# Cross-attention and gated-attention block on one core: a new instruction order on all five engines, with the column-strip products of two groups side by side

## What is computed

```python
def _L0_xattn_ref(x_q, x_kv, indices, W_q, W_kv_down, W_kv_up, W_out):
    q = (x_q @ W_q.T).reshape(b, nq, H, HD)          # 16 heads of 16
    c_kv = x_kv @ W_kv_down.T
    c_sel = c_kv[jnp.arange(b)[:, None, None], indices]   # 64 picks of 154 keys a row
    kv = (c_sel @ W_kv_up.T).reshape(b, nq, K, 2, H, HD)
    scores = jnp.einsum('bqhd,bqkhd->bqkh', q, kv[:, :, :, 0]) * SCALE
    attn = jax.nn.softmax(scores, axis=2)
    return jnp.einsum('bqkh,bqkhd->bqhd', attn, kv[:, :, :, 1]).reshape(b, nq, d) @ W_out.T
...
    # second layer: q1, k1, v, q2, k2 (softmax), gates gk1, gk2 (log-sigmoid / 16), router e
    o = o_dense + o_sparse      # chunked gated linear attention, dense and by expert (4, top 1)
    g = (x @ Wga @ Wgb).reshape(B, L, H, DV)
    o = o * lax.rsqrt(jnp.mean(o * o, axis=-1, keepdims=True) + EPS) * norm_w
    return (o * (g * jax.nn.sigmoid(g))).reshape(B, L, H * DV) @ Wo
x = x + _L0_xattn_ref(_layernorm(x, axis=-1), ctx_1024, itok_BxSx64_0_2047, ...)
x = x + _L0_ffn_ref(_layernorm(x, axis=-1), ...)
```

## Time and profile before

| | |
|---|---|
| median of 3 runs | 1111.31 us (1107.6 to 1114.18) |
| the profiled execution, its own time | 1110.09 us |
| its span, first to last instruction | 1108.8 us |
| mean granted TensorE clock | 0.982 |
| TensorE busy | 1052.0 us, 95% |
| VectorE busy | 956.1 us, 86% |
| ScalarE busy | 898.9 us, 81% |
| GpSimd busy | 698.4 us, 63% |

### The profile page before, as it was taken

The page is one execution under the profiler, slowest core; times in us unless marked ns, Lnnn a source line. Parts: engine busy times, 40 slices in busy tenths (PEclk is TensorE's granted clock), DMA queues, the critical chain, the costliest instruction groups (busy, mean ns, idle before and its releaser), DMA issues.

```text
span 1108.8 us, 36916 instructions
## 1 busy us (share of the span) xinstructions
PE 1052.0 (95%) x14912; PEld 871.9 (79%) x14912; DVE 956.1 (86%) x2793; ACT 898.9 (81%) x2259; POOL 698.4 (63%) x707
## 2 busy tenths in 40 slices
PE   4779999999999999999999999999999999999986
PEld 2557888888888888888888888888888888888764
DVE  5679999998999898999989989998999999998652
ACT  3478888888888888888888888888888888888762
POOL 5356666677765666776666667666667766665554
PEclk8689999999999999999999999999999999999999
DMA  6342322232222222223212222222222222121111
GB/s 199 104 127 59 75 55 63 54 87 63 66 69 52 58 67 67 64 67 89 57 47 62 64 63 73 75 61 67 61 57 68 59 70 59 49 60 50 32 32 25
DMA packets 86880, 74.21 MB, mean 67 GB/s; under 512 B 34553, under 2 KB 71743, under 8 KB 86710
## 3 DMA queue, kind: packets, MB, share of 16 engines
q1 hardware_dynamic: 86134, 70.85, 24.2%
q10 hardware_dynamic: 576, 1.02, 0.3%
HBM read 37.43 MB, written 13.94 MB: 46 GB/s over the span
## 4 chain that ended last, share of the span: by engine, by line
PE 73%; DVE 8%; DMA 5%; ACT 4%; POOL 4%; SPq 3%; issue 2%
PE F L410 9%; PE F L873 5%; PE TM L734 5%; PE F L818 5%; PE F L404 5%; PE F L884 4%; PE F L846 4%; PE F L786 4%; PE F L801 3%; PE F L878 3%; PE TM L743 3%; PE F L759 3%; PE F L829 2%; PE F L865 2%; PE SA L722 2%; PE TM L753 2%
## 5 line engine op out<-in xcount | busy, mean ns | idle before, releaser
L729 DVE CUSTOM_DVE_ANT_0 SA<-SA,LNC 128x154 f32<-128x154 f32 x512 | 146.4, 348 | 12.1 <-PE SA L722 12.1
L2128 POOL TENSOR_TENSOR LS<-LS,ZABS 128x512 f32<-128x512 f32 x27 | 47.4, 1755 | 152.0 <-ACT ZABS L1823 152.0
L734 PE MATMUL TM<-CONST,EXPS 128*128 128x128 f32 x512 | 90.0, 299 | 3.8 <-ACT OT L1735 2.3
L715 DVE TENSOR_REDUCE PACKED<-HOT 128x20 int32<-128x1280 bf16 (+1 forms) x64 | 91.7, 1433 | 0.0
L734 PEld LDWEIGHTS TM<-CONST,EXPS 128*128 128x128 f32 x512 | 72.0, 208 | 17.0 <-issue 12.8
L2118 POOL TENSOR_TENSOR LS<-LS,ZABS 128x1024 f32<-128x1024 f32 x27 | 63.9, 2365 | 33.0 <-ACT ZABS L1889 33.0
L729 DVE DVE_READ_ACCUMULATOR2_ANT MAXS<- 128x1 f32 x512 | 72.2, 141 | 0.0
L2143 POOL TENSOR_TENSOR QM<-QD,ISEXPT 128x1024 f32<-128x1024 f32 x27 | 64.1, 2373 | 5.9 <-DMA QD<-QG 5.9
L722 PE MATMUL SA<-KNOW,QS 128*128 128x154 bf16 x512 | 56.5, 233 | 11.0 <-DMA QS<-q_dram 5.9
L2145 POOL TENSOR_TENSOR AT<-AT 128x1024 f32<-128x1024 f32 x27 | 64.4, 2384 | 3.8 <-DVE AT L1460 3.8
L873 PE MATMUL F<-QM,STATE 128*32 128x128 f32 x2048 | 64.0, 278 | 2.5 <-POOL QM L2183 1.9
(11 more groups left out here) (536 smaller groups left out, 3796.8 us busy)
## 6 DMA issues: line engine op xcount, KB each, us to landing
QD<-QG SPq DMA_DIRECT2D x128, 128.0 KB, 2.3
QS<-q_dram SPq DMA_DIRECT2D x64, 192.0 KB, 3.0
q_dram<-QPARTS SPq DMA_DIRECT2D x32, 192.0 KB, 2.5
XA<-x_dram SPq DMA_DIRECT2D x32, 128.0 KB, 2.1
QS<-q_dram SPq DMA_DIRECT2D x32, 128.0 KB, 3.0
XB<-x_dram SPq DMA_DIRECT2D x32, 128.0 KB, 3.4
out_dram<-OUT SPq DMA_DIRECT2D x32, 128.0 KB, 1.7
EG<-EGP SPq DMA_DIRECT2D x128, 4.0 KB, 1.8
```

The costliest lines, as they stand in the source:

```text
L715: return dve.tensor_reduce(PACKED[:, r], HOT[:, r, :], AX.X, ALU.add)
L729: last = dve.tensor_tensor_reduce(s, s, LNC[t % 2][:, :], -1.0, LARGE, ALU.add, ALU.min, out[:, h:h + 1])
L734: pe.transpose(TA[:, cols(hh)], exps[:, 0:P, hh], ident)
```

## The change

No operation is added, removed or altered. The queues of all five engines are written in a new order, in the first, the middle and the last turns, and the semaphores and waits are drawn anew for it. The diff is 1,444 lines; this is its core, for the middle turns. On TensorE, lines that only rename a semaphore left out:

```diff
         def pe_tiles(l, a, b, c, d, e):
+            pe.wait_ge(s_d_q1, d + 1)
+            gate_products(LS3[d % 2], CUME[d % 2]).then_inc(s_d_g2_ps, 1)
             pe.wait_ge(s_c_xm, c + 1)
-            pe.wait_ge(s_a_xt, c + 3)
             transposes(C0, XM[:, :], KD).then_inc(s_c_xmt_ps, 1)
-            gate_products(LS3[d % 2], CUME[d % 2]).then_inc(s_d_g2_ps, 1)
+            pe.wait_ge(s_b_exps, 4 * b + 1)
+            exp_transposes(EXPS[:, 0]).then_inc(s_b_exps_ps, 1)
             scores(b, 1).then_inc(s_b_b, 1)
...
             hidden(XMT[c % 2]).then_inc(s_c_hidden_ps, 1)
-            exp_transposes(EXPS[:, 0]).then_inc(s_b_exps_ps, 1)
             pe.wait_ge(s_d_q2, d + 1)
             inner(KG1T, Q1).then_inc(s_d_a1_ps, 1)
...
+            pe.wait_ge(s_b_probs, 2 * b + 1)
+            exp_transposes(EXPS[:, 1]).then_inc(s_b_exps_ps, 1)
             pe.wait_ge(s_d_kg2_at1, 2 * d + 1)
-            exp_transposes(EXPS[:, 1]).then_inc(s_b_exps_ps, 1)
+            pe.wait_ge(s_b_exps_2, b + 1)
+            scores(b, 3).then_inc(s_b_b_3, 1)
             pe.wait_ge(s_d_kg2_at1, 2 * d + 2)
...
-            pe.wait_ge(s_b_exps_4, b + 1)
-            scores(b, 3).then_inc(s_b_b_3, 1)
...
             values_pair(b, 2).then_inc(s_b_values, 1)
-            pe.wait_ge(s_c_rt, c + 1)
-            pe.wait_ge(s_c_zmin, 2 * c + 2)
+            pe.wait_ge(s_d_0, d + 1)
+            dense_kv_products(V[d % 2]).then_inc(s_d_kvd_ps, 1)
+            pe.wait_ge(s_c_router_y, 2 * c + 2)
+            pe.wait_ge(s_c_zmin, c + 1)
             router_rows().then_inc(s_c_rows_ps, 1)
+            pe.wait_ge(s_d_sq, d + 1)
+            pe.matmul(D2, const("pairs"), RMS[:, :], start=True, stop=True).then_inc(s_d_ms_ps, 1)
+            pe.wait_ge(s_b_ot, 2 * b + 2)
+            transposes(TA, flat(OT[:, :, :]), GROUPS).then_inc(s_b_ot_ps, 1)
...
+            half_pairs_rows(MIDS, KIDS, WG, HID2, HIDG, WKB, HID1, HIDK).then_inc(s_c_k2_ps, 1)
...
             scores(a, 0).then_inc(s_b_scores, 1)
...
-            dense_kv_products(V[d % 2]).then_inc(s_d_ms_ps_kvd_ps, 1)
...
-            half_pairs_rows(MIDS, KIDS, WG, HID2, HIDG, WKB, HID1, HIDK).then_inc(s_c_k2_ps, 1)
```

On VectorE the K2 product goes ahead of QG2 and the weighting of HOT behind both; of the state halves, half 0 (bank D1) is added first, and LABB comes behind both:

```diff
+            dve.wait_ge(s_c_soft, 6 * d + 5)
+            dve.tensor_tensor(K2[d % 2][:, :, :], K2[d % 2][:, :, :], KS[:, 3, :].unsqueeze(2).to_broadcast([P, H, DK]), ALU.mult).then_inc(s_c_soft, 1)
             dve.wait_ge(s_d_q2_ps, d + 1)
             dve.scalar_tensor_tensor(two_halves(flat(QG2[:, :, :])), MIDD, DK ** -0.5, two_halves(EP[:, :]), ALU.mult, ALU.mult).then_inc(s_d_q2, 1)
...
             dve.wait_ge(s_d_o_ps, d + 1)
+            dve.tensor_tensor(state_half(0), state_half(0), F[:, 2, :], ALU.add).then_inc(s_d_0, 1)
+            dve.tensor_tensor(state_half(1), state_half(1), F[:, 3, :], ALU.add).then_inc(s_d_states, 1)
+            dve.tensor_copy(LABB[:, :], RT[:, 4:5]).then_inc(s_c_router_y, 1)
```

On ScalarE the copy of VM (0, 0) goes to the turn's start, and the fourth EXPS of the second group stands between HID1 and ZPARTS. On GpSimd, of the lane to `state_outputs`:

```diff
+            pool.wait_ge(s_d_egd, 64 * d + 64)
+            decays(d).then_inc(s_d_dec, 1)
             pool.wait_ge(s_c_zparts, 2 * c + 1)
             pool.tensor_tensor(ZREST[:, :], HID2[:, :], ZPARTS[:, 0, :], ALU.subtract).then_inc(s_c_zrest, 1)
```

and X1B is copied before SG, not behind it. On SP:

```diff
             z_slabs(0).then_inc(s_c_zslabs, 16)
+            sp.wait_ge(s_a_qrest, 2 * a + 2)
+            sp.dma_start(q_dram.rearrange("(n p) w -> p n w", n=PARTS), QPARTS[:, :, :, :].rearrange("p n k t -> p n (k t)")).then_inc(s_a_qstore, 16)
             z_slabs(1).then_inc(s_c_zslabs, 16)
             z_slabs(2).then_inc(s_c_zslabs, 16)
```

More of the change, by code:

```diff
@@ L1083, in pe_tiles @@
             values_pair(b, 2).then_inc(s_b_values, 1)
-            pe.wait_ge(s_c_rt, c + 1)
-            pe.wait_ge(s_c_zmin, 2 * c + 2)
+            pe.wait_ge(s_d_0, d + 1)
+            dense_kv_products(V[d % 2]).then_inc(s_d_kvd_ps, 1)
+            pe.wait_ge(s_c_router_y, 2 * c + 2)
+            pe.wait_ge(s_c_zmin, c + 1)
             router_rows().then_inc(s_c_rows_ps, 1)
+            pe.wait_ge(s_d_sq, d + 1)
+            pe.matmul(D2, const("pairs"), RMS[:, :], start=True, stop=True).then_inc(s_d_ms_ps, 1)
+            pe.wait_ge(s_b_ot, 2 * b + 2)
+            transposes(TA, flat(OT[:, :, :]), GROUPS).then_inc(s_b_ot_ps, 1)
+            pe.wait_ge(s_c_hidk, 16 * c + 16)
+            pe.wait_ge(s_c_hidg, 16 * c + 16)
+            pe.wait_ge(s_c_by_label, c + 1)
+            half_pairs_rows(MIDS, KIDS, WG, HID2, HIDG, WKB, HID1, HIDK).then_inc(s_c_k2_ps, 1)
             if a % TPB == 0:
@@ L1090, in pe_tiles @@
             scores(a, 0).then_inc(s_b_scores, 1)
-            pe.wait_ge(s_d_sq_norm, 2 * d + 1)
-            pe.wait_ge(s_d_states_0, 2 * d + 1)
-            pe.matmul(D2, const("pairs"), RMS[:, :], start=True, stop=True).then_inc(s_d_ms_ps_kvd_ps, 1)
-            pe.wait_ge(s_b_ot, 2 * b + 2)
-            transposes(TA, flat(OT[:, :, :]), GROUPS).then_inc(s_b_ot_ps, 1)
-            pe.wait_ge(s_d_states_0, 2 * d + 2)
-            dense_kv_products(V[d % 2]).then_inc(s_d_ms_ps_kvd_ps, 1)
-            pe.wait_ge(s_c_hidk, 16 * c + 16)
-            pe.wait_ge(s_c_hidg, 16 * c + 16)
-            pe.wait_ge(s_c_by_label_scan0, 2 * c + 1)
-            half_pairs_rows(MIDS, KIDS, WG, HID2, HIDG, WKB, HID1, HIDK).then_inc(s_c_k2_ps, 1)
             pe.wait_ge(s_b_out, 2 * b + 2)
@@ L1128, in pe_last_tiles @@
                 hidden(XMT[c % 2]).then_inc(s_c_hidden_ps, 1)
+            if b < TILES:
+                exp_transposes(EXPS[:, 0]).then_inc(s_b_exps_ps, 1)
             if d < TILES:
@@ new lines, in sp_first_tiles @@
+            sp.dma_start(XA[:, :], x[rows(l), :]).then_inc(s_l_load_xa, 16)
+            if l >= 1:
+                sp.wait_ge(s_a_index, l)
+            sp.dma_start(IDX[:, :], idx[rows(l), :]).then_inc(s_l_load_idx, 16)
+            if d >= 0:
+                sp.wait_ge(s_d_exp2, 2 * d + 1)
+                eg_move(d, 0, 1).then_inc(s_d_egd, 16)
+            if b == 0:
+                sp_weights2()
+            if d >= 0:
+                eg_move(d, 0, 0).then_inc(s_d_egd, 16)
+            if a == 0:
+                sp_after_first()
@@ L2225, in sp_first_tiles @@
             if c >= 0:
-                sp.dma_start(HIDK[0:DK, :], HID1[DK:P, :]).then_inc(s_c_hidk, 16)
+                sp.wait_ge(s_c_zstore, 32 * c + 32)
+                z_slabs(2).then_inc(s_c_zslabs, 16)
+            if a == 0:
+                sp_k_store_first()
+            if d >= 0:
+                sp.dma_start(QD[DK * 1:DK * 1 + DK, 0, :, :], QG2[DK * 0:DK * 0 + DK, :, :]).then_inc(s_d_qd, 16)
+            if c >= 0:
+                z_slabs(0).then_inc(s_c_zslabs, 16)
+                z_slabs(1).then_inc(s_c_zslabs, 16)
             if a >= 0:
@@ L2316, in sp_last_tiles @@
+                sp.dma_start(HIDK[0:DK, :], HID1[DK:P, :]).then_inc(s_c_hidk, 16)
                 sp.wait_ge(s_c_zrest, 2 * c + 2)
```

1420 lines of the change are left out of this document (694 added, 726 removed).

## The result

The changed kernel takes 1112.61 us (median of 20 runs, 1110.6 to 1120.39) against 1110.19 for the kernel before in the same comparison (1106.71 to 1114.18): ratio 1.0025, interval 1.0014 to 1.0036. It is slower by 2.4 us. That is less than the 0.5% (5.5 us) which the prediction took for the least that can be told from no change, but with 20 runs of each kernel the interval lies above 1: a small loss. The profiled execution has a span of 1111.9 us (1113.25 in all); its mean granted clock is 0.986, before 0.982, so the loss is not one of the clock.

The account below looks back on a forecast made before the run. TensorE, busy 95% of the span, was taken as the bound. 27 turns at −0.02 to +0.07 us give 0 ± 2; less 1 for the head, 1110.09 becomes 1109, rounded to 1110 us, range 1099 to 1127.

Parts of the forecast that it names:

- The seam: TensorE's cost of entering or leaving 32-column strip products; moving dense kv makes three into two, saving 0.13 us a turn.
- ffn_out to the turn's first group: TensorE segment closing the turn: gates ahead of XM's transposes hide the 0.26 us XM wait, 6.71 to 6.45 us.
- Start to the first inner product: TensorE segment opening the turn: EXPS transposes and gates earlier, new 0.12 us wait for QG, 5.02 to 4.79 us.
- First inner to state_outputs: TensorE segment: same groups reordered, some 0.2 us wait for GpSimd's second QM, 12.58 to 12.8 us.
- the slower rival: GpSimd's lane before state_outputs has no slack, so lateness is paid in full: 0.6 us a turn, 1126 us, chance 0.36.
- State outputs' end to ffn_out: TensorE segment: dense waits for D1, router for LABB, so the mean square starts later; 4.89 to 5.23 us.
- Sum of an undisturbed turn: Five TensorE segments of one steady main-loop turn added: 32.18 us against 32.11 before, +0.07.
- Irregular turns: Turns carrying extra waits: late QS loads gain 1.9 us of room, ZS waits count none; 0 to 0.1 us better.
- QS: Two late loads, 0.35 us each, before TensorE's scores; moving scores (a, 0) two groups later gives them 1.9 us more.
- Head: First turns: q loads no longer stand behind SP's W store; 1 us gained, bounds 0 and 5.
- Tail: Last five turns: counted at nothing, bounded by 1 us to either side.
- Signs: What the new profile would show if right: period 32.1 to 32.3 us, no XM wait, waits on LABB and OG.

Follow-up runs that it names:

- b_dense: Kernel before with only dense_kv_products moved directly behind values_pair(b, 2) and VectorE adding state half 0 first: 1120.46 us, ratio 1.0099.
- experiment 4: Changed kernel with DEC behind ZREST on GpSimd: 1112.82 us; the same with SyncE's middle turns in the old order: 1105.15 us.
- a_sp: Changed kernel with only SyncE's middle turns put back into their order of before: 1105.29 us, ratio 0.9955.
- a_qidx: Changed kernel with q_store behind the third ZS load and the IDX load ahead of the EG moves: 1107.76 us, ratio 0.9987.

## Why the prediction came out as it did, step by step

- **The seam**: 0.13 us a turn forecast; b_dense shows 0.13. Right, and its fate as well ("this is where the saved seam goes"). The estimate of 0.22 us a seam that the prediction drew from the Trainium skill, TensorE: Matmul & The Clock Gate, section Single matmul latency, was too high here. The prediction also feared, by the Trainium skill, TensorEngine Tiling (Array Packing), section PSUM Bottleneck, that emptying PSUM would hold the moved group back. No trace here shows that: dense starts 0.90 us (b_dense) and 0.89 us (changed kernel) after the state outputs' end, right behind the values groups, and the 0.1 us of wait for D1 that the prediction gave it is not there. What b_dense lost came behind dense, from the later mean square.
- **ffn_out to the turn's first group**: 6.45 forecast, 571.77 − 565.29 = 6.48. Right; no wait for XM is left.
- **Start to the first inner product**: 4.79 forecast, 4.99 measured. The wait for QG, put at 0.12, is 0.3 (543.39 to 544.70 less the 1.00 of hidden; TensorE's weights wait for QG 6.1 us in 18 turns). The term was mis-sized by 0.2. The four maxima were put at 0.48 us behind the start of scores (541.45); they start 0.85 behind it, because VectorE is still at the step before:

```profile
541.74 0.65 DVE L1429 TENSOR_SCALAR KS<-KS,RT 128x8 f32<-128x8 f32 x1
542.30 0.31 DVE L729 CUSTOM_DVE_ANT_0 SA<-SA,LNC 128x154 f32<-128x154 f32 x1
```

- **First inner to state_outputs**: 12.8 forecast, 12.64 measured. The second QM, expected to set the end, was done at 557.08, 0.26 us ahead:

```profile
554.70 2.38 POOL L2138 TENSOR_TENSOR QM<-QD,ISEXPT 128x1024 f32<-128x1024 f32 x1
```

 In the earlier trace rows it had been 0.49 ahead. The lane came closer, as said, but did not become the bound: the slower rival, at 0.6 us a turn, did not happen, and taking off DEC's waits brought nothing (experiment 4).
- **State outputs' end to ffn_out**: 5.23 forecast, 5.04. The order of events is the forecast one: dense directly behind L747, LABB late before the router. The sizes: the router starts 1.52 after the state outputs, not 1.66. LABB itself ends when forecast, and I had added 0.20 for the hand-over where 0.05 was seen (561.57 + 0.15 to 561.77):

```profile
560.37 0.69 DVE L1474 TENSOR_TENSOR STATE<-STATE,F 128x512 f32<-128x512 f32 x1 [0.35 <-PE F L878]
...
561.57 0.15 DVE L1476 CAST LABB<-RT 128x1 bf16<-128x1 f32 x1
```

 The chain from mean square to ffn_out, put at 3.30, is 3.27 (565.29 − 562.02), and 3.31 in b_dense.
- **Sum of an undisturbed turn**: 32.18 forecast, 32.06 measured, 32.11 before. The segments' errors, +0.03, +0.20, −0.16 and −0.19, partly cancel; that the sum comes nearer than its terms is partly luck.
- **Irregular turns: the step that failed.** The sum has ZS at nothing: "no wait of before shows ZS, and I count none". It was 4.4 us in 25 turns, and by a_sp SyncE's order cost 6.7 us with the EXPS delays and the first middle turn. The prediction saw that q_store goes between the ZS loads and that the margin shrinks, and didn't measure the margin, though the trace held it: 3.9 us from the last ZS issue to z_features in the turn shown. In the late turns 2.0 to 2.8 pass from issue to use; q_store's issue and the other pieces moved ahead take 1.3, and next to nothing is left for a slow issue of 1.4. It did not name the IDX load between the EG moves at all; a_qidx shows its place to be worth 2.5 to 3.6 us on top of q_store's 1.3 to 2.4. By which wait IDX acts stays open.
- **QS**: gone, as forecast.
- **Head**: −1 forecast, bounds 0 and 5. The first gates come 4.5 us earlier (80.63 against 85.16), inside the bounds, and only 0.4 earlier at index 7 (183.37 against 183.80): 2.5 us are lost in the two turns of the first functions and 1.6 in the first middle one, of which SyncE's order has 1.2. Net almost nothing; the three turns had not been walked.
- **Tail**: nothing forecast; 119.6 us against 120.4.
- **Signs**: no wait for XM, as said. The period of 32.1 to 32.3 was missed by a little on both sides: 32.06 undisturbed, 32.36 at the mean. The waits on LABB and OG did come, but smaller than the 0.1 to 0.3 and the 0.3 or more that were named: TensorE's weights wait 0.16 us a turn for each.

In sum: an ordinary turn was forecast to 0.12 us, and the 1 us that the head was to win did not come. The loss came from turns that aren't ordinary, whose new waits the prediction put at nothing. That the time still lies so near the forecast has a second reason that it did not foresee: the gain of the four computing engines (5 us by a_sp) and SyncE's loss (7) nearly cancel. That is luck.

## What to carry to other kernels

Measure the slack of each transfer from its issue to its first user, in the old trace, before its place in a queue is changed: a wait of zero says nothing of how near it is, and an issue that now and then takes 1.4 us more finds any transfer that has none. When a reordering of all queues brings nothing, put back one queue at a time: here the four computing engines had gained some 5 us, and the queue that only issues transfers lost 7. And the price of a move read in the old order (dense, +11 us) need not be its price in the new one (there it does not delay the router), since what hides it has moved too.

## What the runs showed of the hardware

- SyncE's issue of one and the same transfer takes 0.59 us in one turn and 2.00 in another. Of SyncE's 810 issues 24 stand 1.2 us or more in the kernel before and 21 in the changed one, where the median is 0.47, on many kinds of transfers (XA, EG, QD, QS, HIDK and others). What causes it was not tested.
- The last load of ZS was in use 2.0 to 2.8 us after its issue in the eight turns of the changed kernel in which TensorE stood waiting for it.
- Executions of the same first instructions are granted different clocks: 0.77 to 0.94 from 30 to 60 us, and the first gates start at 81.3 to 77.1 us.
- VectorE's small count extractions still take 1.1 to 1.2 us now and then (0.18 to 0.26 at the median), as in the earlier trace rows, but mostly in another line (L1470) and in 13 of the 27 middle turns, where it was 20 before. In each of these 33 cases the extraction ends 0.04 or 0.05 us after GpSimd's product with SG does: the one in the turn shown stands until 559.59, L2145 until 559.55. That one did not reach TensorE.

```profile
558.38 1.21 DVE L1470 TENSOR_SCALAR COUNTI<-PACKED 128x39 int32<-128x39 int32 x1
```

```profile
558.25 1.30 POOL L2145 TENSOR_TENSOR SG<-SG,LS 128x512 f32<-128x512 f32 x1
```
